# The last layer norm of a decoder layer: a ring of four slots against a whole residual held, half of it normalised on GpSimd

## The reference

```
def _layernorm(x, axis=-1, eps=1e-05):
    m = jnp.mean(x, axis=axis, keepdims=True)
    v = jnp.var(x, axis=axis, keepdims=True)
    return (x - m) / jnp.sqrt(v + eps)
...
    x = _layernorm(x + _L0_attn_ref(...), axis=-1)
    x = _layernorm(x + _L0_xattn_ref(...), axis=-1)
    x = _layernorm(x + _L0_ffn_ref(...), axis=-1)
    return x
```

## Time and profile before

| | us |
|---|---|
| median of 3 runs | 3640.21 (3639.7 to 3642.63) |
| the profiled execution | 3623.67 |
| its span, first to last instruction | 3621.70 |
| `last_norm`, from its first load to the end of the span | 65.0 (from 3556.7) |
| in it: DVE busy | 40.9 |
| in it: ACT busy | 9.9 |
| in it: GpSimd busy | 0.1 |

### The profile page before, as it was taken

The page is one execution under the profiler, slowest core; times in us unless marked ns, Lnnn a source line. Parts: engine busy times, 40 slices in busy tenths (PEclk is TensorE's granted clock), DMA queues, the critical chain, the costliest instruction groups (busy, mean ns, idle before and its releaser), DMA issues. The chain is left out here.

```text
span 3621.7 us, 63739 instructions
## 1 busy us (share of the span) xinstructions
PE 3162.4 (87%) x18589; PEld 2035.1 (56%) x18589; DVE 2182.0 (60%) x4857; ACT 1384.8 (38%) x3155; POOL 1553.3 (43%) x1113
## 2 busy tenths in 40 slices
PE   7998989999899998989796999999788882999990
PEld 4444444454444444444344777776676671888880
DVE  3645556455564645556354788886566662777775
ACT  1443434434354443434322556664000001444441
POOL 3352434424244342434531333342366664666661
PEclk8999999989999999999898999998899996999995
DMA  4122121222203122120283112121321212898996
GB/s 120 40 68 72 33 69 39 68 72 53 78 14 87 48 68 72 31 58 18 86 271 116 58 62 68 62 62 47 106 58 52 60 51 85 232 254 252 248 254 208
DMA packets 189332, 343.99 MB, mean 95 GB/s; under 512 B 36153, under 2 KB 54714, under 8 KB 188090
## 3 DMA queue, kind: packets, MB, share of 16 engines
q1 hardware_dynamic: 132922, 242.51, 23.5%
q0 software_dynamic: 28800, 48.43, 5.9%
q10 hardware_dynamic: 27392, 50.34, 3.8%
HBM read 206.96 MB, written 83.89 MB: 80 GB/s over the span
## 5 line engine op out<-in xcount | busy, mean ns | idle before, releaser
L544 ACT ACTIVATE sa_probs<-sa_s 128x512 f32<-128x512 f32 (+3 forms) x1280 | 615.0, 537 | 747.5 <-PE sa_s L435 414.8
L329 POOL TENSOR_TENSOR sa_both<-sa_probs 128x2048 f32<-128x2048 f32 (+2 forms) x160 | 589.6, 3685 | 696.0 <-PE sa_pv L462 684.5
L401 PE MATMUL sa_w<-sa_parts 96*128 96x512 f32 (+3 forms) x1280 | 518.9, 457 | 115.6 <-DVE sa_pmax L603 34.8
L435 PE MATMUL sa_s<-sa_parts 128*128 128x512 f32 (+3 forms) x1280 | 459.7, 410 | 18.9 <-ACT sa_probs L544 13.7
L607 DVE TENSOR_REDUCE sa_pmax<-sa_w 128x1 f32<-128x512 f32 (+3 forms) x768 | 419.3, 584 | 87.7 <-PE sa_w L401 84.4
L401 PEld LDWEIGHTS sa_w<-sa_parts 96*128 96x128 f32 x1280 | 238.4, 197 | 408.0 <-issue 119.8
L603 DVE CUSTOM_DVE_ANT_0 sa_w<-sa_w,sa_maskS 128x512 f32<-128x512 f32 (+3 forms) x512 | 326.3, 649 | 230.9 <-PE sa_w L401 224.5
L435 PEld LDWEIGHTS sa_s<-sa_parts 128*128 128x128 f32 x1280 | 244.5, 195 | 130.5 <-ACT sa_probs L544 64.4
L1384 POOL DMA_INDIRECT token_and_weight_of_slot<-rt_entry,rt_sl x256 | 254.7, 995 | 142.5 <-issue 74.9
L453 PE MATMUL sa_pv<-sa_probs,sa_values 128*32 128x512 f32 (+3 forms) x2560 | 275.7, 549 | 0.0
L1202 ACT ACTIVATE xa_sm<-xa_sm,xa_nmax 128x154 f32<-128x154 f32 x512 | 208.8, 410 | 64.6 <-DVE xa_nmax L1146 64.6
(11 more groups left out here) (240 smaller groups left out, 5786.5 us busy)
## 6 DMA issues: line engine op xcount, KB each, us to landing
ex_w<-in_w SPq DMA_DIRECT2D x138, 512.0 KB
sa_parts<-sa_halves SPq DMA_DIRECT2D x384, 128.0 KB, 2.5
sa_xt<-in_xT SPq DMA_DIRECT2D x32, 1024.0 KB
scratch_attention_T<-sa_oT SPq DMA_DIRECT2D x32, 256.0 KB, 2.2
on_at<-scratch_attention_T SPq DMA_DIRECT2D x32, 256.0 KB, 3.3
on_xr<-in_x SPq DMA_DIRECT2D x32, 256.0 KB, 3.3
scratch_x<-on_xn ACTq DMA_DIRECT2D x32, 256.0 KB, 2.1
scratch_x_T<-on_xnT ACTq DMA_DIRECT2D x32, 256.0 KB, 3.3
```

Source lines behind the costliest of these rows:

```text
L329: pool.tensor_tensor(both[:, :, 0:w], probs[:, even, :, 0:w], probs[:, odd, :, 0:w], ALU.add).then_inc(both_ready, 1)
L401: nc.tensor.matmul(ps[:, 0:w], qparts[0:3 * HD, h, q0:q0 + P], kparts[0:3 * HD, h, k0:k0 + w], start=True, stop=True).then_inc(work_ready, 1)
L435: mm = nc.tensor.matmul(ps[:, 0:w], kparts[:, h, kb * P:(kb + 1) * P], qparts[:, h, q0:q0 + w], start=True, stop=not diag)
L544: nc.scalar.activation(probs[:, r % NPB, h, 0:w], sbank[n % NSB][:, 0:w], ACT.Exp).then_inc(exp_done, 1)
```

## The change

`r`, `stats`, `mv`, `std` and `rstd` get 16 places for pairs instead of 4, so the whole residual lies in SBUF (64 KB of each partition). SyncE issues its 16 loads in a row. `rows` gives partition p the rows 2p and 2p + 1 of a pair, one piece of 4 KB in DRAM; the same for the store. DVE normalises the first tile of a pair and GpSimd the second, both after the same reciprocal, and ACT's store waits for both. There are no loops any more: all engines run straight code, and DVE and ACT keep one pair ahead through all 16 pairs. The stores count on one semaphore. The other stages are as they were.

```diff
--- before.py
+++ after.py
@@ -1910,83 +1910,80 @@

 def last_norm(nc, sems, res, out):
     PAIR = 2
-    RING = 4
-    ROUNDS = NT // PAIR // RING
+    PAIRS = NT // PAIR
     with ExitStack() as ctx:
         def sb(name, shape, dt=F32):
             return ctx.enter_context(nc.sbuf_tensor("ln_" + name, shape, dt))

         sem = ctx.enter_context(own_semaphores(nc, "ln_"))
         passed = sem("passed")
-        r = sb("r", [P, RING, PAIR, DM]); stats = sb("stats", [P, RING, PAIR, 6]); mv = sb("mv", [P, RING, PAIR, 2])
-        std = sb("std", [P, RING, PAIR]); rstd = sb("rstd", [P, RING, PAIR]); eps = sb("eps", [P, 1])
-        consts = sem("consts"); r_in = [sem(f"r_in{i}") for i in range(RING)]; stats_done = sem("stats_done")
-        mv_done = sem("mv_done"); std_done = sem("std_done"); rstd_done = sem("rstd_done"); o_done = sem("o_done")
-        o_out = [sem(f"o_out{i}") for i in range(RING)]
+        r = sb("r", [P, PAIRS, PAIR, DM]); stats = sb("stats", [P, PAIRS, PAIR, 6]); mv = sb("mv", [P, PAIRS, PAIR, 2])
+        std = sb("std", [P, PAIRS, PAIR]); rstd = sb("rstd", [P, PAIRS, PAIR]); eps = sb("eps", [P, 1])
+        consts = sem("consts"); r_in = [sem(f"r_in{i}") for i in range(PAIRS)]; stats_done = sem("stats_done")
+        mv_done = sem("mv_done"); std_done = sem("std_done"); rstd_done = sem("rstd_done")
+        first_done = sem("first_done"); second_done = sem("second_done"); o_out = sem("o_out")
         block = ctx.enter_context(nc.Block())

         def rows(dram, t):
-            return dram[bass.ds(t * (PAIR * P), PAIR * P), :].rearrange("(n p) d -> p n d", p=P)
+            return dram[t * (PAIR * P):(t + 1) * (PAIR * P), :].rearrange("(p n) d -> p n d", p=P)

         @block.sync
         def _(sp):
-            for s in range(RING):
-                sp.dma_start(r[:, s], rows(res, s)).then_inc(r_in[s], 16)
-            with sp.Fori(1, ROUNDS) as i:
-                for s in range(RING):
-
-                    sp.wait_ge(o_out[s], i * 16)
-                    sp.dma_start(r[:, s], rows(res, i * RING + s)).then_inc(r_in[s], 16)
+            for t in range(PAIRS):
+                sp.dma_start(r[:, t], rows(res, t)).then_inc(r_in[t], 16)

         @block.gpsimd
         def _(pool):
             pool.memset(eps[:], EPS).then_inc(consts, 1)
+            for t in range(PAIRS):
+                pool.wait_ge(rstd_done, t + 1)
+                apart(pool, passed)
+                pool.tensor_scalar(r[:, t, 1], r[:, t, 1], mv[:, t, 1, 0:1], rstd[:, t, 1:2], ALU.subtract,
+                                   ALU.mult).then_inc(second_done, 1)

         @block.scalar
         def _(act):
             act.wait_ge(consts, 1)
-            def deviation(t, s):
+
+            def deviation(t):
                 act.wait_ge(mv_done, t * PAIR + PAIR)
-                nc.scalar.activation(std[:, s], mv[:, s, :, 1], ACT.Sqrt, bias=eps[:]).then_inc(std_done, 1)
-
-            def store(t, s):
-                act.wait_ge(o_done, t * PAIR + PAIR)
-                act.dma_start(rows(out, t), r[:, s]).then_inc(o_out[s], 16)
-
-            with act.Fori(0, ROUNDS) as i:
-                deviation(i * RING, 0)
-                for s in range(RING):
-                    if s + 1 < RING:
-                        deviation(i * RING + (s + 1), s + 1)
-                    store(i * RING + s, s)
-            for s in range(RING):
-                act.wait_ge(o_out[s], 16 * ROUNDS)
+                nc.scalar.activation(std[:, t], mv[:, t, :, 1], ACT.Sqrt, bias=eps[:]).then_inc(std_done, 1)
+
+            def store(t):
+                act.wait_ge(first_done, t + 1)
+                act.wait_ge(second_done, t + 1)
+                act.dma_start(rows(out, t), r[:, t]).then_inc(o_out, 16)
+
+            for t in range(PAIRS):
+                deviation(t)
+                if t > 0:
+                    store(t - 1)
+            store(PAIRS - 1)
+            act.wait_ge(o_out, 16 * PAIRS)

         @block.vector
         def _(dve):
-            def measure(t, i, s):
-                dve.wait_ge(r_in[s], i * 16 + 16)
+            def measure(t):
+                dve.wait_ge(r_in[t], 16)
                 for n in range(PAIR):
-                    dve.bn_stats(stats[:, s, n], r[:, s, n]).then_inc(stats_done, 1)
+                    dve.bn_stats(stats[:, t, n], r[:, t, n]).then_inc(stats_done, 1)
                 for n in range(PAIR):
                     dve.wait_ge(stats_done, t * PAIR + (n + 1))
                     apart(dve, passed)
-                    dve.bn_aggr(mv[:, s, n], stats[:, s, n]).then_inc(mv_done, 1)
-
-            def normalise(t, s):
+                    dve.bn_aggr(mv[:, t, n], stats[:, t, n]).then_inc(mv_done, 1)
+
+            def normalise(t):
                 dve.wait_ge(std_done, t + 1)
-                dve.reciprocal(rstd[:, s], std[:, s]).then_inc(rstd_done, 1)
+                dve.reciprocal(rstd[:, t], std[:, t]).then_inc(rstd_done, 1)
                 dve.wait_ge(rstd_done, t + 1)
-                for n in range(PAIR):
-                    dve.tensor_scalar(r[:, s, n], r[:, s, n], mv[:, s, n, 0:1], rstd[:, s, n:n + 1], ALU.subtract,
-                                      ALU.mult).then_inc(o_done, 1)
-
-            with dve.Fori(0, ROUNDS) as i:
-                measure(i * RING, i, 0)
-                for s in range(RING):
-                    if s + 1 < RING:
-                        measure(i * RING + (s + 1), i, s + 1)
-                    normalise(i * RING + s, s)
+                dve.tensor_scalar(r[:, t, 0], r[:, t, 0], mv[:, t, 0, 0:1], rstd[:, t, 0:1], ALU.subtract,
+                                  ALU.mult).then_inc(first_done, 1)
+
+            measure(0)
+            for t in range(PAIRS):
+                if t + 1 < PAIRS:
+                    measure(t + 1)
+                normalise(t)

 
 def program(nc, t):
```

## The result

| | before | changed |
|---|---|---|
| median of 3 runs, us | 3640.21 (3639.7 to 3642.63) | 3621.37 (3615.4 to 3622.4) |
| the profiled execution, us | 3623.67 | 3621.37 |
| its span, us | 3621.7 | 3619.6 |
| first load of `last_norm`, us | 3556.7 | 3571.7 |
| `last_norm`, first load to the end, us | 65.0 | 47.9 |

The ratio of the times is 0.9942 (95% interval 0.9919 to 0.9965): 18.8 us faster by the medians, where 17.1 were forecast; the forecast was 3623.1. The profile of before is of an execution of its own, 3623.67, which is none of the three; that of after is the execution at the median.

The account below looks back on a forecast made before the run. The ring of four slots bounds the kernel; with loads freed, bytes end the section at 3604.6, later than the engines' 3601.5. That is 17.1 us off: 3640.2 - 17.1 = 3623.1 us, range 3619 to 3632.

Parts of the forecast that it names:

- What bounds the kernel before: In the last section, the ring of four slots: load, statistics, normalise, store, and only then the next load.
- DVE's pace without its second tile, 2.16 us: DVE in the last section: a pair takes 2.62 us, less 0.46 without the second TENSOR_SCALAR, so 2.16 us.
- The engine bound, 3601.5: Section end by engines: DVE's last instruction 3595.9, GpSimd's lag 0.9, way out 4.7; 20.2 us earlier than 3621.7.
- The rate of the mix, 375 GB/s with bounds of 330 and 400: DMA rate with loads and stores together in the last section: 13.5 MB left take 36.0 us at 375 GB/s.
- the bytes bound: Section end by DMA bytes: 3604.6, 17.1 us earlier, and 3.1 us later than the end by engines.
- Part 2: Two neighbouring rows per partition, 4 KB pieces on load and store: counted at nothing, above that 1 to 2 us gain.
- Part 3: GpSimd normalises every second tile: taken at 0.75 us each, between 0.61 and 1.27, with 2.16 us until the next.
- Part 4: Straight code without branches and register steps: counted at nothing; fetching longer code 0 to 2 us, taken at 0.
- Behind the waiting store stands only the next deviation, which DVE needs a whole pair later: On ACT: a store waiting for GpSimd's half hides between queued stores; at the end it shows, within the 0.9 us.
- Rival C: DVE and GpSimd hinder each other, a pair costing 2.77 to 3.43 us: gain 11.4 to 0.8 us; chance 0.08.
- Rivals B and D: Slow DMA mix: B at 330 GB/s, gain 12.2 us, chance 0.25; D at 211 GB/s, 10.9 us later, chance 0.03.
- E: SyncE's queue takes only a few loads at a time, so loads don't run ahead; no time of its own.

Follow-up runs that it names:

- the kernel with ACT: Changed kernel with each pair's second tile normalised by ACT, GpSimd computing only the bias: section 44.9 us, ratio 0.9948; repeated, 45.1 us, 0.9945.
- the bytes alone: Changed kernel without any engine's work on the rows, each pair stored once landed: section 45.0 us with 4 KB pieces, 47.2 with 2 KB.

## Why the prediction was right, and where it was not

*What bounds the kernel before:* right. Of what DVE waited for loads after the first, 13.2 us by the earlier trace rows, both tiles on DVE with loads free left 0.3 and took 14.0 us off, with the same tile work on the same engine. The straight code and the larger pieces have no kernel of their own on the ring, so they may hold a little of the 14.0.

*DVE's pace without its second tile, 2.16 us:* right, shown by the kernel with ACT (2.16), in the changed kernel 2.22. With both tiles it is 2.61, as in the earlier trace rows: the forecast of 50.9 for that kernel came out at 51.0.

*The engine bound, 3601.5, which is 44.8 us of section:* 3.1 too low. From its first statistics to its last instruction DVE took 36.7 us for 34.6, 2.15 more: the pace, up to 16 x 0.06 = 1.0; waits for ACT, 0.21 and 0.52 in the timeline above, 0.7; and the gap of 0.23. GpSimd's end behind DVE's was 2.7 for 0.9, 1.8 more. Against that the way in was 4.3 for 4.6 and the way out 4.15 for 4.7, together 0.85 less. The sum is 3.1.

*The rate of the mix, 375 GB/s with bounds of 330 and 400:* the term that was mis-sized most for the outcome. It is 420 to 422, above both bounds, and the bytes bound is 45.0 and not 47.9. DVE's waits for loads in the later part, which the forecast worked out from it, didn't come. The windows of before that I averaged had the start of a mix in each of them; only the one at 409 showed the steady state, and that with pieces of 2 KB, where 408 is the steady rate.

*Part 2, pieces of 4 KB counted at nothing:* its size was wrong in the bytes (2.2 us). Within the change, where the engines set the end, it was right to some tenths: 0.6 to 0.9 us, all of them ahead of the first statistics. The two rows at 397 GB/s didn't show it.

*Part 3, GpSimd's half at 0.75 us with bounds 0.61 and 1.27:* wrong by nearly three times, 2.07 alone. This is the step that failed. The bounds were other instructions of that size, a copy and one with two inputs; a two-operation TENSOR_SCALAR lies beyond both, and neither was a bound. With it the limit that counts changed: GpSimd's lag at the end and its share in the pace lifted the engines' end above the 45.0 us of the bytes. "Has 2.16 us until the next" was then no margin but a coincidence: 2.07 just fits, 2.23 doesn't.

The Trainium skill, page GPSIMD Engine Reference, section 4.1 (Engine selection), puts an operation with one input at roughly line rate. Its copy at 610 ns fits that, the TENSOR_SCALAR at 1.56 us with one operation and 2.07 with two doesn't; the measurement decides.

*Part 4, straight code at nothing:* no price shows but one small gap. Before the reciprocal of the 13th pair DVE stood for 0.23 us with nothing that the profile shows to wait for (3606.26), at the same place in both profiles of the changed kernel and of the one with ACT, and not with both tiles on DVE. Its cause isn't shown.

*"Behind the waiting store stands only the next deviation, which DVE needs a whole pair later":* true for most pairs, and wrong at the end, where DVE has no statistics between and waited 0.52 us for a deviation that stood behind a store that waited for GpSimd.

*Rival C, getting in each other's way:* it exists, but small. The argument against it, that DVE is in first, was wrong for most pairs, though. It held for the first, where DVE began at 3579.54 and GpSimd at 3579.73. After that GpSimd had one gap only, of 0.19 us, and as its instruction takes as long as a pair, DVE began its own 0.3 us before GpSimd was done with the pair before. The argument had GpSimd beside the statistics only, and hung on the 0.75 us too. What it cost was small all the same: DVE's TENSOR_SCALAR took 0.62 for 0.55, GpSimd's 2.23 for 2.07, and neither was held up until the other's end, as DVE was at 2187.32 in the earlier trace rows. Both together stretch a pair by 0.06 us, not by 0.61 to 1.27. Why it is so much less here stays open.
*Rivals B and D:* fell with 420 GB/s. *E:* the queue did fill (issues of up to 1.3 us, the 16 loads all issued within 9.5 us), and it cost nothing.

So the 47.9 us came out by two errors of 3 us that cancelled: the bytes were 2.9 quicker than forecast and the engines 3.1 slower, and the time forecast is that of the later of the two. The sign of the gain, and that most of it comes from the loads, rest on steps that the runs bear out. That the section came out as forecast to 0.1 us, with the wrong one of the two limits, is luck.

## What to carry to other kernels

Where a ring that is reloaded only after its store has landed is the bound, as here, the time that a slot is held counts, and moving work to a slower engine made it worse; free the loads first, and only then share out the work. A window of a DMA rate is a bound for a steady stream only if no start of a stream lies in it. The price of an instruction on GpSimd that no row shows is not bounded by other instructions of the same shape, and an idle ACT at 0.81 us was the better place for this one, by 2.5 to 3.0 us of the section.

## What the runs showed of the hardware that I had not expected

- GpSimd's TENSOR_SCALAR of 128x512 f32: 1.56 us with one operation, 1.92 with two and constants, 2.07 with two and operands per partition, where its copy takes 0.61.
- Loads and stores together reach 420 to 422 GB/s with pieces of 4 KB and 408 with 2 KB, more than the 397 of loads alone in the earlier trace rows, but for three microseconds at the start of the mix only 281 without any engine at work, and 311 to 326 beside the engines' work.

  The Trainium skill, page DMA: Bandwidth & Descriptors, section Bandwidth, gives 435 GB/s as the ceiling of the fabric and says that for transfers between HBM and SBUF the HBM side at about 358 binds. Its table of loads by a single core reaches 425 all the same. On this one core 420 was held for 34 us by the bytes alone (3568 to 3602), near the first figure and above the second.
- In straight code ACT's table load of 1.28 us came once, behind the wait of its first activation: at 3577.72, released by the statistics. The loop of before had one at the start of each of its four rounds, the first at 3557.22, ahead of the wait for the statistics. DVE's wait of 0.21 us for the first deviation stands right behind it.
- The stage with routing scatters by 15 us between executions of the same code, with TensorE's granted clock at 0.93 to 0.95 of full over it. A gain of 0.5% can't be read from one execution's span; it can from the section.
